# Heads stacked in pairs, the choice of experts spread over more steps, and two more expert tiles beside the last batch, in a fused attention and mixture-of-experts kernel

## What is computed

```python
xn = layernorm(x); qp = xn @ Wq.T
idx = argmax(qp @ ctx.T, axis=-1)              # one context row per token
mk, mv = split(ctx[idx] @ Wkv.T)               # 16 wide each, shared by the heads
att = softmax(heads(qp) @ mk.T / 4) @ mv
x = x + tanh(g_xattn) * (att @ Wc.T)
xf = layernorm(x); logits = xf @ gate_w
top_w = softmax(top_2(logits))
out = x + tanh(g_ffn) * sum_e comb[:, e] * (gelu(xf @ w1[e] + b1[e]) @ w2[e] + b2[e])
```

## Time and profile before

| | |
|---|---|
| median of 3 runs | 924.6 us (923.81 to 925.47) |
| the profiled execution | 923.9 us, of which the span from first to last instruction is 922.1 us |
| mean granted TensorE clock | 0.944 of full |
| PE busy | 801.9 us, 87% of the span |
| PEld, DVE, ACT, POOL busy | 547.1 (59%), 521.0 (56%), 370.3 (40%), 427.6 us (46%) |
| pipeline of batches 0 to 6 | seven stretches of 36 to 56 us, from 92.5 to 436.4 us |
| expert loop | about 570 us to the end; PE busy 250.00 of the 250.00 us from 600 to 850 us |

### The profile page before, as it was taken

How to read it: one execution, slowest core, us unless ns; L and a number is a source line. 1 busy time by engine, 2 the same in 40 slices (tenths; PEclk the granted TensorE clock), 3 DMA queues, 4 the chain that set the end, 5 groups by cost and what they waited for, 6 DMA issues and landing times.

```text
span 922.1 us, 20046 instructions
## 1 busy us (share of the span) xinstructions
PE 801.9 (87%) x6326; PEld 547.1 (59%) x6327; DVE 521.0 (56%) x1582; ACT 370.3 (40%) x772; POOL 427.6 (46%) x469
## 2 busy tenths in 40 slices
PE   3785899989897998888778868999999999999994
PEld 1333344435353443443347657899888888899773
DVE  4585576667767567776444873544444544444441
ACT  1222363735435363566653612433333333333331
POOL 4596363755666546443614753333333333333322
PEclk9886899979899898989989989999999999999998
DMA  5554333353624334224425342322222333322300
GB/s 173 129 122 139 60 92 80 117 104 93 128 95 109 64 114 105 69 70 136 138 88 160 54 127 46 59 47 46 44 46 44 55 53 50 48 42 36 44 12 1
DMA packets 62798, 74.64 MB, mean 81 GB/s; under 512 B 6401, under 2 KB 56449, under 8 KB 62593
## 3 DMA queue, kind: packets, MB, share of 16 engines
q1 hardware_dynamic: 49424, 56.74, 24.0%
q0 software_dynamic: 13296, 16.92, 10.7%
HBM read 46.75 MB, written 27.55 MB: 81 GB/s over the span
## 4 chain that ended last, share of the span: by engine, by line
PE 66%; DVE 12%; ACT 6%; issue 6%; POOL 5%; DMA 3%; DVEq 1%; SPq 1%; ACTq 0%; POOLq 0%
PE ps_o L2578 20%; PE ps_d L2562 9%; PE ps_a L2562 9%; PE ps_d L1237 6%; PE ps_o L1317 5%; PE ps_d L1280 3%; PE ps_e L1212 3%; PE ps_e L1342 3%; PE ps_a L1300 2%; PE ps_e L1195 2%; DVE row_max L987 2%; PE ps_r L2548 1%; ACT prob L805 1%; ACT rows L827 1%; PE ps_a L1304 1%
## 5 line engine op out<-in xcount | busy, mean ns | idle before, releaser
L2578 PE MATMUL ps_o<-w_split,hidden 128*128 x1136 | 192.2, 276 | 13.4 <-DVE y L2534 8.4
L805 ACT ACTIVATE prob<-ps_a 128x512 f32<-128x512 f32 x192 | 112.9, 603 | 188.0 <-PE ps_a L1300 109.8
L987 DVE TENSOR_REDUCE row_max<-ps_d 128x2 f32<-128x384 f32 x237 | 127.8, 551 | 58.8 <-PE ps_d L1280 57.4
L2578 PE MATMUL ps_o<-w_split,h_lo 128*128 x568 | 156.6, 276 | 0.0
L2473 POOL DMA_INDIRECT out<-y,token_at x71 | 118.5, 1669 | 42.3 <-POOL token_at L2471 30.9
L2578 PEld LDWEIGHTS ps_o<-w_split,hidden 128*128 128x128 bf16 x1136 | 112.1, 99 | 30.2 <-issue 15.3
L2520 DVE TENSOR_TENSOR h_lo<-hidden 128x512 bf16<-128x512 f32 (+1 forms) x156 | 101.0, 686 | 25.5 <-ACT hidden L2489 24.7
L2534 DVE TENSOR_TENSOR y<-ps_o,b_all 128x512 f32<-128x512 f32 (+1 forms) x39 | 25.1, 644 | 155.6 <-PE ps_o L2578 148.7
L1280 PE MATMUL ps_d<-k_st,w_split 96*128 96x192 bf16 x474 | 84.4, 267 | 26.4 <-DVE row_max L987 19.8
L2562 PE MATMUL ps_a<-x_hi,w_split 128*128 128x256 bf16 (+1 forms) x624 | 104.4, 265 | 0.0
L2562 PE MATMUL ps_d<-x_hi,w_split 128*128 128x256 bf16 (+1 forms) x624 | 103.6, 264 | 0.1
(11 more groups left out here) (242 smaller groups left out, 1307.1 us busy)
## 6 DMA issues: line engine op xcount, KB each, us to landing
w_stage<-w SPq DMA_DIRECT2D x32, 512.0 KB, 4.5
xg<-queue SPq DMA_DIRECT2D x31, 260.0 KB, 2.9
w_split<-q_split SPq DMA_DIRECT2D x24, 256.0 KB, 8.0
x_in<-x SPq DMA_DIRECT2D x8, 512.0 KB, 4.3
ctx_sb<-ctx_t SPq DMA_DIRECT2D x8, 512.0 KB, 3.9
x<-x SPq DMA_DIRECT2D x8, 512.0 KB, 4.3
q_split<-q_hl SPq DMA_DIRECT2D x16, 256.0 KB, 3.4
out<-x SPq DMA_DIRECT2D x8, 512.0 KB, 5.0
```

The costliest lines, as they stand in the source:

```text
L805: a.activation(prob[n % 2][:, j, :], ps_a[i % 2][:], ACT.Exp, scale=SCALE).then_inc(exp_ready, 1)
L987: v.tensor_reduce(row_max[:, t, 2 * pair:2 * pair + 2], bank[:, 0:2 * SLOTS].rearrange("p (h r) -> p h r", h=2), AX.X, ALU.max).then_inc(m ...
L2578: last = nc.tensor.matmul(ps_y[:, t, :], hs[s][:, f, token], k.w2_split[:, bass.ds(e, 1), part, f, :].rearrange("p a d -> p (a d)"), start ...
```

## The change

1. **Two-head stacks.** Partitions 0 to 48 hold an even head's rows and 64 to 112 an odd head's, with four rows for the maxima behind (117 in all). The keys are stored twice in one operand of 384 columns per batch, 192 for the even head (odd rows nil) and 192 for the odd one. A row-maximum tile is one matmul of 384 columns and not two of 192. The last 64 slots of the two heads stand in adjacent columns, so their logits are one matmul of 128 columns instead of two of 64. The stack takes six transfers of 128 KB instead of three of 256 KB, `packed_keys` three activations instead of one, and GpSimd prepares `k_st` at the start.
2. **EARLY** is 8 instead of 6, with `EARLY_BATCHES` still 6: TensorE loads two more expert numbers, and waits for the last weight piece, before tile 6.
3. **The choice of experts** starts a step later (`turn_rows` 25, its copies 26, `gates` 27, copy 28, `turn_gate` 29). DVE's part is split: `top_two` at step 30, `choose` at 31. The ratio comes at 31, `rank` at step 0 of the next p, `queue_slots` and the scatter at 1. `shares` goes from DVE to POOL step 31, with a power of -1 for the reciprocal. Three more matmuls add the earlier tiles' sums to the ranks, and `queue_slots` has six operations instead of eleven, two of them behind the signal to the scatter.
4. **W_TWO** is (12, 14) instead of (14, 28).

```diff
-EARLY = 6
+EARLY = 8
-        PE_TURN_HEADS, PE_OUT, PE_TURN_ROWS, PE_TURN_MAX, PE_GATE, PE_TURN_GATE, PE_RANK = 8, (10, 12), 24, 26, 26, 28, 31
+        PE_TURN_HEADS, PE_OUT, PE_TURN_ROWS, PE_TURN_MAX, PE_GATE, PE_TURN_GATE, PE_RANK = 8, (10, 12), 25, 26, 27, 29, 0
-        W_TWO = (14, 28)
+        W_TWO = (12, 14)
...
                 for c, part in enumerate((0, 1, 0)):
-                    sp.dma_start(q_st[s % 3][c * DH:(c + 1) * DH], k.q_split[s, part].rearrange("(h r) l -> r h l", h=H)
-                                 ).then_inc(q_loaded, 16)
-                sp.wait_ge(q_loaded, 48 * (s + 1))
+                    queries_of = k.q_split[s, part].rearrange("(h odd r) l -> odd r h l", odd=2, r=DH)
+                    for odd in range(2):
+                        sp.dma_start(q_st[s % 3][odd * ODD + c * DH:odd * ODD + (c + 1) * DH], queries_of[odd]
+                                     ).then_inc(q_loaded, 16)
+                sp.wait_ge(q_loaded, 96 * (s + 1))
...
+            def shares(e):
+                pool.wait_ge(ratio_ready, e + 1)
+                chain.step(g.tensor_copy(rows[:, :, D + 3], token[:]))
+                chain.then(g.tensor_scalar(share[:], ratio[:], 1.0, None, ALU.add))
+                chain.then(g.tensor_tensor(share[:], share[:], minus_one[:], ALU.pow))
...
             def queue_slots(e):
                 dve.wait_ge(ranked, e + 1)
...
+                chain.step(v.tensor_tensor(queue_end[:], ps_rank.rearrange("p (t e) -> p t e", t=LT),
+                                           queue_next[:, None, :].to_broadcast([P, LT, E]), ALU.add))
+                chain.then(v.tensor_reduce(queued[:], ps_tile.rearrange("p (t e) -> p e t", t=LT), AX.X, ALU.add))
...
-                for c in range(2):
-                    last = t_.matmul(ps_da[n][:, c * SLOTS:(c + 1) * SLOTS],
-                                     q_st[m % 3][0:ROW_MAX, 2 * pair + c, t * P:(t + 1) * P],
-                                     k_st[0:ROW_MAX, m % 3, :], start=True, stop=True)
-                last.then_inc(logits_b_ready, 1)
+                t_.matmul(ps_da[n][:, 0:2 * SLOTS], q_st[m % 3][0:PAIR_ROWS, pair, t * P:(t + 1) * P],
+                          k_st[0:PAIR_ROWS, m % 3, :], start=True, stop=True).then_inc(logits_b_ready, 1)
...
-                t_.matmul(ps_rank, k.before[:], both, start=True, stop=True)
+                t_.matmul(ps_rank, k.before[:], both, start=True, stop=False)
+                for t in range(1, LT):
+                    t_.matmul(ps_rank[:, t * E:], k.ones_bf[:], both[:, 0:(LT - t) * E], start=False, stop=(t == LT - 1))
                 t_.matmul(ps_tile, k.ones_bf[:], both, start=True, stop=True).then_inc(ranked, 1)
```

More of the change, by code:

```diff
@@ L290, in flow @@
 def flow(nc, k, sem, sb, ps, block):
+    half = W_EACH // 2
     with ExitStack() as own:
@@ L691, in deviation @@
                 g.tensor_tensor(rstd[:, 1, :], variance[:, 1, :], minus_half[:], ALU.pow).then_inc(rstd_ready, 1)
+            def shares(e):
[3 more added lines that the diff above has]
+                chain.then(g.tensor_tensor(share[:], share[:], minus_one[:], ALU.pow))
+                chain.then(g.tensor_scalar(share[:], share[:], k.tanh_g[:, 1:2], None, ALU.mult))
+                chain.step(g.tensor_copy(rows[:, :, D], share[:]))
+                chain.step(g.tensor_tensor(rows[:, :, D + 1], share[:], ratio[:], ALU.mult))
+                chain.then(g.tensor_scalar(token[:], token[:], float(L), None, ALU.add))
             def scatter(e):
@@ L725, in _ @@
                     scatter(e - 1)
+                if step == POOL_SHARES and is_batch(e):
+                    shares(e)
                 for i in pieces(p, step, 1):
@@ L735, in _ @@
                     deviation(LAST)
+                if step == END_SHARES:
+                    shares(LAST)
                 if step == END_QUEUE:
@@ L918, in _ @@
             v.memset(v_st[:], 0.0)
[L919 to L922 removed]
+            v.memset(k.w_split[0:PAIR_ROWS, Q_AT[0], 0:half].bitcast(F32), TWO_ONES)
+            chain.then(v.memset(key_cols[:, :, ROW_PAD:P], 0.0))
+            for at in (ROW_PAD, ODD + ROW_PAD):
+                chain.step(v.memset(key_cols[:, :, at:at + 1], 1.0))
+            v.memset(key_cols[:, :, PAIR_ROWS + 2:PAIR_STACK], 1.0).then_inc(dve_ready, 1)
             dve.wait_ge(dve_ready, 2)
@@ L925, in _ @@
             dve.wait_ge(tanh_ready, 1)
+            chain.step(v.tensor_copy(queue_next[:], k.queue_at[:]))
             chain.then(v.memset(gate_wide[:], 0.0))
@@ L1098, in queue_slots @@
                 dve.wait_ge(slots_ready, e + 1)
+                chain.step(v.tensor_tensor(queue_next[:], queue_next[:], queued[:], ALU.add))
+                chain.then(v.tensor_tensor(k.n_queued[:], k.n_queued[:], queued[:], ALU.add))
             n_d = 0
@@ L1132, in _ @@
                     copy_max(m)
+                if step == DVE_TOP and is_batch(e):
+                    top_two(e)
                 if step == DVE_CHOOSE and is_batch(e):
                     choose(e)
-                if step == DVE_SHARES and is_batch(e):
-                    shares(e)
                 if step == DVE_QUEUE and is_batch(e - 1):
@@ L1426, in _ @@
                     turn_gate(e)
-                if step == PE_RANK and is_batch(e):
-                    rank(e)
+                if step == PE_RANK and is_batch(e - 1):
+                    rank(e - 1)
+                if step == STEPS - 1 and p == LAST:
+                    rank(LAST - 1)
                 if step == PE_EXPERTS and p == LAST:
                     pe.wait_ge(k.tables_ready, 2)
-                    expert = [k.load_expert(pe, i) for i in range(EARLY)]
+                    expert = [k.load_expert(pe, i) for i in range(EARLY_BATCHES)]
                 if step == PE_EARLY and p == LAST:
@@ L1464, in _ @@
                         bank_da[n].wait_read(pe)
+                    if (i, n) == (EARLY_BATCHES, 0):
+                        pe.wait_ge(w_lo, N_PIECES)
+                        expert += [k.load_expert(pe, more) for more in range(EARLY_BATCHES, EARLY)]
                     k.layer1(pe, i, n, None, expert[i])
```

126 lines of the change are left out of this document (64 added, 62 removed).

## The result

The changed kernel takes 915.31 us (median of 20 runs, 912.06 to 923.87) against 924.78 us before (922.97 to 926.25): a ratio of 0.9913, 95% interval [0.9894, 0.9932]. It is faster, as forecast, but by 9.5 us where 22 were forecast. The time lies in the range; the size of the gain does not lie near the forecast.

The account below looks back on a forecast made before the run. TensorE was taken to bound the kernel, except where DVE holds it up behind the choice, with clock drops following; -6.5 - 6.5 + 1.7 - 9 - 1.7 = -22.0 from 923.9 gave 902 us, range 887 to 919.

Parts of the forecast that it names:

- Two-head stacks: Last-slot logits on TensorE: eight per batch save 0.11 us each, -6.5 us in all, between 0 and -9.
- Choice of experts: DVE's work per batch: 2.9 us saved, less 1.0 and 0.5, taken as 1.3; five batches -6.5 us.
- The wait at the gates: TensorE's `gates` wait for ACT's copies: 1.45 us per batch, between 0 and 2.6, making step 28 about 1 us later.
- the first rival: TensorE's clock comes back wholly, 14 us: 897 us, or 890 with no wait at `gates`; chance 0.22.
- The fourth rival: Slower: the `gates` wait makes its own low-clock stretch, 3.5 us each, 935 us in seven batches; chance 0.08.
- Clock: TensorE's lower-level stretches behind the choices shrink from 37.70 us, a third staying: -9 us, between 0 and -14.
- Start-up: First stack's six transfers delay the load of x behind them: +1.7 us, between 0 and +3.5.
- Tail: TensorE's 6.99 us stall before the early tiles' last layer shrinks as DVE comes 1.1 + 0.7 us sooner: -1.7.
- EARLY as 0: Two more early tiles move from the loop to before it at the same TensorE rate: 0 us.
- A power on GpSimd as 0: `shares` brings a 1.03 us power to GpSimd beside DVE's `choose` or `queue_slots`; holds nothing, costed at 0.

Follow-up runs that it names:

- e7: Changed kernel with ACT's two copies of the turned rows first in step 26 and an early signal for the keys: 900.45 us, 0.9734 of before.
- e14: Kernel before with the new choice of experts and the weight pieces moved, no two-head stacks, EARLY 6: 914.42 us, 0.9918 of before.
- e15: The changed kernel run once more, nothing altered: 914.44 us, 0.9903 of before.
- e8: Changed kernel with EARLY back at 6: 912.76 us, 0.9873 of before.
- e5: Changed kernel with ACT's two copies of the turned rows first in step 26: 905.01 us, 0.9787 of before.
- e13: Kernel before with the new choice of experts, weight pieces moved and ACT's copies first, no two-head stacks, EARLY 6: 905.15 us, 0.9804 of before.
- e9: Kernel before with the new choice of experts alone and ACT's two copies first in step 26: 912.30 us, 0.9864 of before.
- e3: Kernel before with the two-head stacks alone: 924.32 us, 0.9995 of before.
- e1: Kernel before with only the weight pieces moved, W_TWO = (12, 14): 922.57 us, 0.9964 of before.
- e2: Kernel before with the new choice of experts alone; stacks, EARLY and W_TWO as before: 924.38 us, 0.9973 of before.
- e10: Changed kernel with ACT's copies first, the keys' early signal and EARLY at 6: 898.93 us, 0.9717 of before.

## Why the prediction was wrong

The direction and the range held; the sum did not: 9.5 us instead of 22. What failed is the price of the two waits that the change makes: that for the packed keys was put at nothing, and that at the gates at 1.0 us in five batches, 5 us. In the profile they are 6.2 and 9.2 us. Without the second, and with half of the first, the time falls by 14.9 us (e7), 9.9 more than the 5 that had been netted, and 12.5 were missing. That e7's 900.45 us lie beside the forecast of 902 is in part luck: its terms, as measured below, differ from the forecast ones both ways. By its steps:

- **Two-head stacks: a failed step.** "8 x 0.11" per batch, -6.5 us, measured 0 as made together with EARLY (e14 against e15), and at most some 4 without (e14 against e8). There are two errors in it. "The two further activations of `packed_keys` delay ACT by about 0.8, which `turn_rows` at 25 and row maxima at 25 can just bear" was wrong: the tile of step 25 waits for them and for the copies behind them, 1.04 us on the mean of the five batches from 140 to 400 us, which the full-clock windows of e14 and of the changed kernel show as 14.23 to 15.01. And "where TensorE is the pacer" was wrong for most of the batch: 0.77 us of work saved shortened the stretch by 0.30. The Trainium skill ("TensorEngine Tiling (Array Packing)", Key Properties) names the drain at a change of tiling mode. The rows agree that the pairs are dearer, 0.34 against 0.23 us, though no run parts the drain from the cost of a second matmul, and PE's busy time fell; but a saving on an engine that then waits is no time.
- **Choice of experts: right in sign at the full clock.** The forecast was 1.3 us per batch, with the pieces' 1.07 in it, so some 0.2 without. The choice added to the pieces gives 14.78 to 14.23, 0.55, from one stretch of each profile. The wait at the gates, forecast at 1.45 and measured at 1.31, is 14.23 to 13.02, 1.2 us.
- **The wait at the gates: the other failed step.** I netted it at 1.0 us in five batches, and the first rival at 5 x 1.45 = 7.25. It falls in seven, and is 2.0 us in the last. Removing it gave 10.3 us in e5, where 8.0 us of it went, and 9.3 in e13 against e14. These are the waits of e14 and of e13:

```profile
PE ps_e L1366 <- ACT turned L854: 9.9, 7, 2.0
```

```profile
PE ps_e L1366 <- ACT turned L854: 1.2, 2, 0.8
```

  So most of the gain is the wait's own length, in all batches; the rest may be the clock. The low clock does not go with this wait alone: of the five stretches one is low in e5 where four were, but three in e13 against four in e14, and all five in e9. The fourth rival's mechanism is there at a smaller price: a stretch at 0.90 of the clock costs 15.49 - 14.23 = 1.26 us, not 3.5, and it replaced the old low stretch instead of being added to it.
- **Clock: near its size in time at the lower level.** I forecast that a third of 37.70 us would stay, 13 us, so that 25 come back. The five choices and the stretches between them, before and with the change:

```profile
176.29:405.51 229.22, 201.93 (x1385) 97.32 (x1384) 160.73 (x531) 108.10 (x217) 127.75 (x146) 0.91 0.39 96
```

```profile
177.06:398.03 220.97, 191.79 (x1225) 86.45 (x1223) 146.97 (x471) 110.50 (x225) 137.59 (x180) 0.95 0.35 97
```

  By the clock column of the single windows, some 41 us of the first and 20 of the second are at the lower level (17 in e15, of 219.38 us): 21 to 24 came back. But the whole is only 8.3 us shorter, 9.8 in e15, where the choice (6.5), five batches of stacks (4.5) and the clock (9) were to give 20. At the forecast's own price the clock accounts for this by itself; no run measures that price apart. By that price the two terms that do not hang on the clock gave next to nothing here, as the two new waits took them back. With these out, one stretch of five is low (e7), and the time, 900.45, is nearer the forecast of 902 than the 890 that the first rival gave for no wait at the gates.
- **Start-up: right in size, perhaps by luck.** The first logits come 1.6 us later, and 1.7 was forecast, but the six transfers are 0.4 of it (0.5 in e3). Where the rest comes from was not tried; e1 and e2 show it without new stacks, and it lies within the spread of the profiles.
- **Tail: right in its term, not in its sum.** The stall ahead of the early tiles' last layer fell from 6.99 to 3.7 us, more than the 1.7 forecast (whose own terms, 1.1 + 0.7, are 1.8). But from step 4 of batch 7 to the end the profiled run took 485.6 us against 483.1 before, with more time at the low clock there; e15 took 481.8. EARLY as 0: not contradicted beyond the noise.
- **A power on GpSimd as 0: right.** It does not hold an operation of DVE with two inputs in SBUF; the rows of the changed kernel in one batch:

```profile
429.47 1.03 POOL L717 TENSOR_TENSOR share<-share,minus_one 128x4 f32<-128x4 f32 x1
```

```profile
429.95 0.23 DVE L1129 TENSOR_TENSOR is_choice<-is_choice,queue_end 128x64 f32<-128x64 f32 x1
```

  The rule of the Trainium skill ("SBUF — State Buffer", Who interferes with whom) lets whichever of the two starts first hold the port. Here, as far as GpSimd's spans tell, which are rough, DVE started 0.48 us into the power, and took its usual 0.22 to 0.23, so this pair speaks against the rule, as the earlier trace rows do, and the batch around 470.9 us shows it again. At the gap the rule agrees. `either` starts 0.01 us ahead of the power in four of the five batches before, and 0.04 behind it in the other, and takes 0.19 to 0.20 us in all.

## What to carry to other kernels

When a change moves work to a later step, write down for each engine what then stands ahead of it in that step, and price the wait that this makes in every batch in which it falls. Here that was most of its cost; what the clock does behind it came on top, and one profile of a kernel does not tell how much. An order within a step can be worth more than the change: two moved lines and one semaphore gave 14.9 us here, the change itself 9.5. A saving on the busiest engine counts only in stretches where no wait ends later; a window without the part in question, compared at an equal clock, shows how much of it arrives.

The version that combines all of this, e10 (the change, with ACT's copies first, the keys' signal and EARLY at 6), takes 898.93 us, 0.9717 [0.9699, 0.9735] of the kernel before.

## What the runs showed that I had not expected

- The same program spreads by the clock: the changed kernel's runs go from 912.06 to 923.87 us with mean clocks from 0.962 to 0.946, while the 29 runs of before beside e1 and its fellows stayed within 922.7 to 926.8.
- An activation on ACT has a cost that hardly falls with its size: those of 64x192, 53x128 and 53x64 last 0.51, 0.44 and 0.40 us. Three took 1.27 us from first start to last end, where one of 98x192 took 0.54.
